# Rows of C by four DMAs each, and attention's probabilities turned over 128 rows and columns

## The reference

```python
# L0, attention in windows of 49 pixels, 4 heads of 8
attn = softmax(einsum('whnd,whmd->whnm', q, k) * scale)
out  = einsum('whnm,whmd->whnd', attn, v)      # then a projection

# L1, the recurrence of the Mamba block, state n of 8, over the 784 pixels of an image
h = exp(d_t[..., None] * A) * h + (d_t * u_t)[..., None] * b_t[:, None, :]
y_t = einsum('bdn,bn->bd', h, c_t)
```

## Time and profile before

| what | value |
|---|---|
| median of 3 runs | 427.69 us (424.73 to 428.63) |
| the profiled execution | 426.04 us, span 424.3 us, mean granted TensorE clock 0.977 |
| busy | PE 368.8, DVE 306.4, ACT 286.9, POOL 166.5 us |
| chain of work that ended last | PE 38%, DVE 24%, issue 16%, ACT 9%, POOL 8%, DMA 3% |
| DMA issues of `Cs` | 32, of 392 KB each |
| DMA issues of `SX` | 16, of 336.8 KB each |

### The profile page before, as it was taken

How to read it: one execution, slowest core, us unless ns; L and a number is a source line. 1 busy time by engine, 2 the same in 40 slices (tenths; PEclk the granted TensorE clock), 3 DMA queues, 4 the chain that set the end, 5 groups by cost and what they waited for, 6 DMA issues and landing times.

```text
span 424.3 us, 11081 instructions
## 1 busy us (share of the span) xinstructions
PE 368.8 (87%) x4065; PEld 254.5 (60%) x4065; DVE 306.4 (72%) x631; ACT 286.9 (68%) x600; POOL 166.5 (39%) x142
## 2 busy tenths in 40 slices
PE   5799999999999597989499775998978989999996
PEld 4577777777755243444154342453954579888885
DVE  2869887698664989888269889985758957555554
ACT  3588899999967868759646793359974364444443
POOL 8314132232201438833985899970722400000000
PEclk9969999999999999999979999999999989999998
DMA  7120000002314272462222222200020001111111
GB/s 160 9 21 8 2 3 1 0 0 56 76 28 108 106 175 101 129 160 98 102 103 102 103 80 102 105 12 0 14 65 2 2 1 23 19 20 22 21 22 27
DMA packets 28496, 23.23 MB, mean 55 GB/s; under 512 B 20928, under 2 KB 22720, under 8 KB 28464
## 3 DMA queue, kind: packets, MB, share of 16 engines
q1 hardware_dynamic: 28068, 22.77, 19.8%
q10 hardware_dynamic: 396, 0.05, 0.1%
HBM read 2.00 MB, written 1.61 MB: 9 GB/s over the span
## 4 chain that ended last, share of the span: by engine, by line
PE 38%; DVE 24%; issue 16%; ACT 9%; POOL 8%; DMA 3%; SPq 1%; DVEq 1%; ACTq 1%; POOLq 0%
PE pair L1683 6%; DVE pair L1976 3%; PE pair L1174 3%; POOL hC L542 3%; PE pair L1185 3%; PE pair L1134 3%; DVE stats L1757 3%; PE pair L1299 2%; DVE Ts L1867 2%; PE pair L1193 2%; PE pair L1671 2%; DMA vec<-in_L_conv_b_qkv 2%; PE pair L1156 2%; PE pair L1352 2%; PE pair L1228 2%
## 5 line engine op out<-in xcount | busy, mean ns | idle before, releaser
L542 POOL TENSOR_TENSOR hC<-Hs,Cs 128x784 f32<-128x784 f32 x31 | 59.6, 1929 | 38.4 <-DVE Hs L1988 17.3
L510 POOL TENSOR_TENSOR Km<-Ks,mask 128x784 f32<-128x784 f32 x16 | 24.1, 1508 | 71.0 <-ACT Ks L717 71.0
L1352 PE MATMUL pair<-hC,ident 128*128 128x392 f32 x128 | 48.6, 504 | 1.3 <-POOL hC L542 1.2
L1861 DVE TENSOR_REDUCE mx<-pair 128x8 f32<-128x392 f32 x64 | 33.0, 556 | 19.3 <-PE pair L1134 19.2
L1976 DVE TENSOR_TENSOR pair<-DU,pair 128x392 f32<-128x392 f32 x64 | 35.6, 556 | 15.3 <-PE pair L1348 15.1
L1683 PE MATMUL pair<-hst,BD 128*128 128x112 f32 x224 | 37.7, 299 | 2.1 <-DVE Rt L2241 0.4
L1174 PE MATMUL pair<-ident,Pr 113*113 113x113 f32 x256 | 37.3, 280 | 2.5 <-issue 1.6
L1174 PEld LDWEIGHTS pair<-ident,Pr 113*113 113x113 f32 x256 | 31.2, 184 | 12.8 <-issue 12.0
L1348 PE MATMUL pair<-BCf,sel 96*128 96x392 bf16 x64 | 21.8, 343 | 16.6 <-DVE Hs L1988 9.7
L1988 DVE TENSOR_TENSOR_SCAN Hs<-dA,Hs,pair 128x392 f32<-128x392 f32 x32 | 33.0, 1030 | 3.6
L1683 PEld LDWEIGHTS pair<-hst,BD 128*128 128x128 f32 x224 | 30.0, 195 | 9.1 <-DVE hst L2235 5.2
(11 more groups left out here) (254 smaller groups left out, 840.8 us busy)
## 6 DMA issues: line engine op xcount, KB each, us to landing
Cs<-BCf SPq DMA_DIRECT2D x32, 392.0 KB
SX<-XP SPq DMA_DIRECT2D x16, 336.8 KB, 5.9
XT<-in_x SPq DMA_DIRECT2D x4, 392.0 KB, 7.0
out<-Os SPq DMA_DIRECT2D x28, 56.0 KB, 1.7
AD<-Aa SPq DMA_DIRECT2D x4, 196.0 KB
NB<-in_L_conv_x_proj_w SPq DMA_DIRECT2D x4, 3.0 KB
DW<-in_L_conv_dw SPq DMA_DIRECT2D x4, 1.1 KB
W<-in_L_conv_w_qkv ACTq DMA_DIRECT2D x1, 48.0 KB
```

The lines of the kernel that those rows point to most:

```text
L542: eng.tensor_tensor(hC[:, i % NHC, :], Hs[:, i % NHS, :], Cs[i % NCS][:, :], ALU.mult).then_inc(v_c, 1)
L1352: return eng.matmul(STATES[:, h, :], ident[:, :], src[:, columns(h)], start=first, stop=last)
L1861: eng.tensor_reduce(mx[:, g, :], banks[g][:, 0:392].rearrange("p (m k) -> p m k", k=WT), AX.X, ALU.max).then_inc(max_r, 1)
```

## The change

Two edits.

The DMA of a state's C rows becomes four, one for each group: each reads one partition of BCf, repeated 32 times, and writes 32 partitions of the tile. All waits for `s_cs` count 16 x 4 for a state. The waits ahead of the issue stay.

The transposes take all 128 rows and columns of a pair of blocks, pads included. ScalarE copies 128 partitions of the bank, and the memset of `PT` is gone, as the copy now writes every partition; ScalarE waits for four memsets, not five.

```diff
-KW = WP + 49
@@ c_rows
-                    eng.dma_start(Cs[i % NCS][:, :], bcast(BCf[3 * C + n:P:DS, c % 2, :], 1, C)).then_inc(s_cs[i % NCS], 16)
+                    for g in range(G):
+                        row = 3 * C + DS * g + n
+                        eng.dma_start(Cs[i % NCS][C * g:C * g + C, :], bcast(BCf[row:row + 1, c % 2, :], 1, C)).then_inc(s_cs[i % NCS], 16)
@@ gpsimd
-            for m in (xw, Qw, Vst, Pr, PT):
+            for m in (xw, Qw, Vst, Pr):
@@ times_c
-                    eng.wait_ge(s_cs[i % NCS], 16 * (i // NCS + 1))
+                    eng.wait_ge(s_cs[i % NCS], 16 * G * (i // NCS + 1))
@@ turned_out
-                    eng.activation(PT[0:KW, g].rearrange("p a b (o q) -> p (a b o) q", o=2),
-                                   banks[5 + (par + 1 + g) % 2][0:KW, :].rearrange("p (m k) -> p m k", k=WP)[:, :, 0:WT], ACT.Copy).then_inc(ring_r, 1)
+                    eng.activation(PT[:, g].rearrange("p a b (o q) -> p (a b o) q", o=2),
+                                   banks[5 + (par + 1 + g) % 2][:, :].rearrange("p (m k) -> p m k", k=WP)[:, :, 0:WT], ACT.Copy).then_inc(ring_r, 1)
@@ scalar
-            eng.wait_ge(s_mk2, 5)
+            eng.wait_ge(s_mk2, 4)
@@ transposes
-                        pg = Pr[0:KW, np_, g, 2 * k:2 * k + 2, :].rearrange("p h k -> p (h k)")[:, 0:KW]
-                        ins = eng.transpose(bk[0:KW, P * k:P * k + KW], pg, ident[0:KW, 0:KW])
+                        pg = Pr[:, np_, g, 2 * k:2 * k + 2, :].rearrange("p h k -> p (h k)")
+                        ins = eng.transpose(bk[:, P * k:P * k + P], pg, ident[:, :])
```

More of the change, by code:

```diff
@@ L619, in pool_ssm @@
                     times_c(3, 5, 6)
-                    eng.wait_ge(s_cs[(DS * J - 1) % NCS], 16 * (DS * J // NCS))
+                    eng.wait_ge(s_cs[(DS * J - 1) % NCS], 16 * G * (DS * J // NCS))
                     eng.wait_ge(v_b, 2 * DS * J)
@@ L2072, in _ @@
             c, i = J - 1, DS * J - 1
-            eng.wait_ge(s_cs[i % NCS], 16 * (DS * J // NCS))
+            eng.wait_ge(s_cs[i % NCS], 16 * G * (DS * J // NCS))
             eng.wait_ge(v_s, 2 * DS * J)
```

## The result

The changed kernel takes 469.2 us (median of 4, 468.82 to 469.45), the kernel before 427.6. The ratio is 1.098, with a 95% interval from 1.093 to 1.104. It is slower, inside the range of 433 to 640 and on the side that was forecast. The loss is 42 us where 72 were forecast (500 against 427.7). The profiled span is 467.5 us.

A forecast was written before the change was run, and what follows sets the result against it. The prediction saw no compute engine filling the scan and a nearly back-to-back C-row stream. Span 424.3 + 74 (rows) + 0 (transposes) = 498 us, plus 3.4 to the median, rounded to 500; range 433 to 640.

The forecast's parts named there:

- What bounds the kernel: In the scan no compute engine is full; the nearly back-to-back C-row stream takes 129 of 140.5 us.
- 16 engines for each DMA: In the scan's C-row stream, each new one-row DMA is served by 16 engines, two packets each.
- The rule of leading sizes: For DMAs, engines are the largest number up to 16 dividing the slowest size that isn't 1 on both sides.
- The limit belongs to what is read: In C-row DMAs, the partitions read limit the rate, not the engines; one source partition gives at most 25 GB/s.
- A row costs 4.0 us: In the C stream, one row's 32 packets need 4.0 us however many engines ask; four in step take 16.1 us.
- 2.5 busy sources: In the C stream, engines drift partly apart; the middle between one and four busy sources gives 6.4 us a state.
- The sum: Scan stream: 32 states at 6.4 us plus 14 us for SX, ending at 356.5 us; +74 us after slack.
- SyncE: Four DMA issues for a state in the scan take 1.7 to 2.2 us, covered within 6.4 us, so cost nothing.
- GpSimd's wait: In the scan, GpSimd's wait for Cs grows from 16 to some 80 us.
- The transposes: In attention, transposes of 128 by 128 cost 0 us, bounds -0.6 to +2.6 us, covered by the projection's 0.34 us wait.
- Rival 3: In the scan, packets stay at 0.126 us with 16 engines on one partition; 1.0 us a state, 420 us; chance 0.06.
- TensorE's clock: In the longer scan, the clock may fall from 0.98; given no size, left to the range.

The follow-up runs named there:

- the run with other sources: Changed kernel, but each of a state's four DMAs reads 32 different partitions of US, not one repeated row of BCf: 418.0 us, 0.980 of before.
- in one: Kernel before with the new transposes, one DMA for a state reading 128 different partitions of US: 419.5 us, 0.983 of before.
- DRAM: Kernel before with new transposes, C rows written to DRAM once a step, four copies each, and read back by one DMA a state: 417.9 us, 0.979.
- the run by row: Changed kernel with eight DMAs of 16 partitions for a state, both halves of a row one after the other: 528.8 us, 1.244 of before.
- with one source: Changed kernel, but all four DMAs of a state read the same partition 96 + n: 752.4 us.

## Why the prediction was right, and what was mis-sized

- **What bounds the kernel.** Right. Without the stream on the path, the time is 418 to 420 us in three ways (other sources in four DMAs, in one, and DRAM).
- **16 engines for each DMA.** Right: 16 small packets for each DMA, and 93% of all engines busy. The rule of leading sizes held for 2, 4 and 32.
- **The limit belongs to what is read.** Right, by the run with other sources. It is narrower than the prediction's sum had it, which gave each partition a limit of its own: four neighbouring partitions count as one. The four rows of a state lie eight partitions apart and gave 73 GB/s together, so they don't all share one limit.
- **A row costs 4.0 us.** Mis-sized. I took what one engine draws from a source it has for itself, 25 GB/s, and called it the most. 16 engines draw 28: 3.6 us a row, 14.3 for a state in step, not 16.1.
- **2.5 busy sources.** This was the middle between the ends, which no row gave, and 2.6 was measured: that it came so near was luck. The reason given was drift alone, with three states waiting in the queues. Four DMAs are under way, one state, and the run by row shows that this number counts: 2.0 sources, and 60 us more.
- **The sum.** 14.3 / 2.6 = 5.5 us a state, not 6.4. With that, 135.3 + 32 x 5.5 + 14 = 325 for the end of the stream (326.3 measured), against 356.5. The span would grow by 325 - 278 - 4 = 43, and it grew by 43.2. Against the 74 of the forecast that is a miss of 31 us: 29 in the time of a state, 32 x (6.4 - 5.5), of which the rate of a shared source is 32 x 16.1 / 2.5 - 32 x 14.3 / 2.5 = 23, and 2 in the stream's start at 135.3 and not 137.5. The 14 us for SX were not measured apart, but 191 - 32 x 5.5 = 15 are left for them. Two ends of the range come out by their own terms at 640 for 1.5 sources, not 638, and 444 for 3.5, not 443; nothing hangs on it.
- **SyncE.** I counted 1.7 to 2.2 us a state and called it covered. Unhindered, four issues take 2.4 to 2.6 us (0.59 to 0.65 each, with other sources), and in the changed kernel 5.5 (1.37 each), as long as a state, so that SyncE stands in the chain with 13%. It costs nothing of its own there, as the run with other sources shows.
- **GpSimd's wait.** 66 us where some 80 were named, in line with the shorter stream.
- **The transposes.** Right: no time, with the cover named (0.28 us are left of 0.34). Eight took 0.08 us more where 0.1 was worked out. One more transpose was put at 0.10 us, but the earlier trace rows give (0.96 - 0.65) / 4 = 0.08 at 113, and the changed kernel (1.04 - 0.66) / 4 = 0.10 at 128. The weight load of 141 ns is what the transposes of Zc had shown.
- **Rival 3** had the time without the stream on the path right: 420 us, and 418 to 420 came out. Its premise, that 16 engines on one partition draw 16 times as much, fell with the first trace.
- **TensorE's clock** was left to the range. It fell to 0.85 in the scan. Whether any of the 43 us is due to it was not tried. It can be little: SyncE waited for a free tile 8.8 us in all, so what goes through TensorE hardly held up the stream, and the sum closes without it.

## What to carry to other kernels

Before a broadcast out of SBUF is spread over more DMA engines, count how many of its source partitions lie apart: neighbours count as one, the engines can only share what the sources give, and here 4 engines on 4 sources beat 16 engines that queue on the same four by 27 GB/s. Read the DMA share next to the GB/s: a share that rises while the rate falls is a crowd on one end. If few rows must reach many partitions often, it can pay to write them to DRAM once, with so many copies side by side that a read has 16 leading rows, and to read from there; here the time was 2% under that of the kernel before, though the way there took 6 us.

## What the runs showed of the hardware

- 16 engines draw 28 GB/s from one partition, and as much from four neighbouring ones; one engine alone draws 25 (the kernel before, a source for each of its four).
- With slow transfers only four or five DMAs of SyncE's queue were under way at a time, and the issue itself takes longer: 0.59 us unhindered, 1.30 in the changed kernel, 3.67 with one source (medians).
- Small DMAs back to back cost SyncE 0.64 to 0.65 us each, and with eight for a state that alone is 5.1 us.
- The order of the same 256 DMAs alone moved the time by 69 us (459.4 against 528.8).
- A transpose with 128 rows and columns has a shorter weight load than one with 113 (141 against 179 ns).
